# A graph network's two attention layers: one chain per chunk shared anew between ScalarE and VectorE, and the order of single steps moved

## The reference, cut to what matters

```python
h = jnp.maximum(_layernorm(x), 0.0)
x = x + _L0_gnn_ref(h, adj, embed, layer, embed_bias, layer_bias)
h = jnp.maximum(_layernorm(x), 0.0)
x = x + _L1_gnn_ref(h, adj, beta1, beta2)
# _L0_gnn_ref:
h = h_add(h_mul(x, embed), embed_bias)
neigh = exp_map_zero(adj @ log_map_zero(h))
out = h_add(h_mul(concatenate((x, neigh), 1), layer), layer_bias)
# _L1_gnn_ref, twice, _leaky after each:
x_norm = x / clip(norm(x), EPS)
attn = softmax(where(a > 0, beta[0] * (x_norm @ x_norm.T), NEG_INF))
h = attn @ x
```

## Time and profile before

| | us |
|---|---|
| runs shown | 993.46, 994.92, 997.03 |
| profiled execution | 993.61, its span 992.1 |
| TensorE busy | 935.3 (94%) |
| VectorE busy | 819.4 (83%) |
| ScalarE busy | 511.4 (52%) |
| fp32 products of the aggregation (L463) | 225.6 |

### The profile page before, as it was taken

How to read it: one execution, slowest core, us unless ns; L and a number is a source line. 1 busy time by engine, 2 the same in 40 slices (tenths; PEclk the granted TensorE clock), 3 DMA queues, 4 the chain that set the end, 5 groups by cost and what they waited for, 6 DMA issues and landing times.

```text
span 992.1 us, 22921 instructions
## 1 busy us (share of the span) xinstructions
PE 935.3 (94%) x9024; PEld 698.0 (70%) x9024; DVE 819.4 (83%) x2110; ACT 511.4 (52%) x708; POOL 8.0 (1%) x21
## 2 busy tenths in 40 slices
PE   2789999999997989999999999989999999999996
PEld 1754444444444878788888888768878888888885
DVE  7791888888888987788988898988768788888887
ACT  2720211211216575765656677777565565656564
POOL 0000000000000000000000000000000000000000
PEclk9879999999998999999999999999999999999999
DMA  8219888888881444555555655535655556555630
GB/s 343 94 62 312 278 284 277 278 286 298 275 275 43 168 174 177 207 210 219 211 200 195 244 206 192 183 145 187 238 183 212 211 193 245 213 204 205 252 139 36
DMA packets 29971, 207.26 MB, mean 209 GB/s; under 512 B 3632, under 2 KB 4272, under 8 KB 5296
## 3 DMA queue, kind: packets, MB, share of 16 engines
q1 hardware_dynamic: 28224, 203.44, 56.6%
q0 software_dynamic: 640, 2.10, 0.5%
q10 hardware_dynamic: 1008, 0.33, 0.1%
HBM read 203.75 MB, written 2.10 MB: 207 GB/s over the span
## 4 chain that ended last, share of the span: by engine, by line
PE 84%; DVE 8%; ACT 4%; issue 2%; DMA 1%; DVEq 0%; POOL 0%; SPq 0%; POOLq 0%; ACTq 0%
PE acc_ps L463 20%; PE s_ps L614 17%; PE s_ps L600 10%; PE acc_ps L667 6%; PE acc_ps L663 6%; PE acc_ps L665 6%; PE acc_ps L644 5%; PE acc_ps L640 5%; PE acc_ps L642 5%; PE acc_ps L427 1%; DVE work L1604 1%; ACT work L971 1%; DMA x_sb<-in_x 1%; ACT set L764 1%; PE s_ps L441 1%
## 5 line engine op out<-in xcount | busy, mean ns | idle before, releaser
L971 ACT ACTIVATE work<-s_ps,beta_bias,beta_scale 128x1024 f32<-128x1024 f32 x144 | 173.5, 1205 | 223.2 <-PE s_ps L614 223.2
L463 PE MATMUL acc_ps<-ring,set 128*128 128x512 f32 x512 | 225.6, 600 | 3.1 <-DVE set L1230 3.1
L1622 DVE SCALAR_TENSOR_TENSOR h_all<-ring,s_ps 128x1024 f32<-128x1024 f32 x112 | 136.6, 1220 | 69.9 <-PE s_ps L600 69.1
L463 PEld LDWEIGHTS acc_ps<-ring,set 128*128 128x128 f32 x512 | 97.3, 192 | 120.8 <-issue 117.8
L1604 DVE TENSOR_TENSOR work<-work 128x1024 f16<-128x1024 f32 x96 | 132.5, 1380 | 5.4 <-ACT work L981 5.4
L981 ACT ACTIVATE work<-work 128x1024 f16<-128x1024 f32 x96 | 131.5, 1369 | 3.1
L1612 DVE SCALAR_TENSOR_TENSOR work<-ring,work 128x1024 f32<-128x1024 f32 x96 | 116.7, 1215 | 0.0
L614 PE MATMUL s_ps<-xt 128*128 128x512 f16 x432 | 107.6, 385 | 6.3 <-ACT work L971 5.5
L614 PE MATMUL s_ps<-set 128*128 128x512 f16 x432 | 105.3, 379 | 2.6 <-ACT t L1029 2.1
L663 PE MATMUL acc_ps<-set,work 128*128 128x129 f16 x576 | 103.5, 220 | 4.6 <-DVE accs L1639 2.7
L663 PE MATMUL acc_ps<-src,work 128*128 128x129 f16 x576 | 102.9, 219 | 1.9 <-ACT accs L995 1.9
(11 more groups left out here) (254 smaller groups left out, 1726.1 us busy)
## 6 DMA issues: line engine op xcount, KB each, us to landing
ring<-in_adj_t SPq DMA_DIRECT2D x192, 1024.0 KB, 5.0
x_sb<-in_x SPq DMA_DIRECT2D x4, 512.0 KB, 7.3
out<-x_sb POOLq DMA_DIRECT2D x8, 256.0 KB, 2.5
w<-in_layer ACTq DMA_DIRECT2D x2, 64.0 KB, 8.7
w<-in_embed ACTq DMA_DIRECT2D x1, 64.0 KB, 4.2
eb<-in_embed_bias ACTq DMA_DIRECT2D x1, 64.0 KB, 7.0
lb<-in_layer_bias ACTq DMA_DIRECT2D x1, 64.0 KB, 11.3
beta<-in_beta ACTq DMA_DIRECT2D x2, 0.5 KB, 14.6
```

The costliest lines, as they stand in the source:

```text
L463: last = nc.tensor.matmul(agg, v_sb[:, jb, :], ring[:, k, b, :], start=jb == 0, stop=jb == NB - 1)
L971: nc.scalar.activation(values[x.n % VR], score_ps, ACT.Exp, bias=beta_bias[:, x.la:x.la + 1], scale=beta_scale[:, x.la:x.la + 1]).then_inc ...
L1622: V.scalar_tensor_tensor(turned[x.off % MR].rearrange("p (b j) -> p b j", b=CB), ring[:, x.mir_tile % AR, :, ds(x.h * HB * P, HB * P)], 0. ...
```

## The change

- **Row 0's total.** On ScalarE `first_total` moves ahead of the slot's exponential, and the `first_flush` of the same slot behind it.
- **Row 5** of the first attention layer is turned 11 slots after its last half, not 10.
- **Last chunk.** Its chain is cut for 12 pauses, its slots 0 and 1 stand ahead of its first Tanh on ScalarE, `chunk_scales` has a part of its own, the scaled rows come two slots later, and its columns are turned in slot 12, not 11.
- **Every chunk.** `gnn_chunk` uses the same functions as the last chunk: ScalarE does the squares of t1, relu and its squares, both scaled rows and the high halves, at the end of its part of the chunk; VectorE keeps the small steps and the low halves. VectorE's steps on its own semaphore go from 82 to 77 for each chunk, the asks from 5 to 7.
- **First stage.** The relu pass is gone; the transposes read scr_b, and the copy out of PSUM applies relu. The `gb` products come chunk by chunk behind `g`; `web` is made before the layer norm's scalars. SyncE waits for x before it loads the ring.

```diff
-        LAST_CHUNK_AT = 11
-        turned_at = {LAST_CHUNK_AT: (0, NC - 1), **{rows_of[a].last + 10: (1, a) for a in range(NC)}}
+        LAST_CHUNK_AT = 12
+        turned_at = {LAST_CHUNK_AT: (0, NC - 1), **{rows_of[a].last + (11 if a == 5 else 10): (1, a) for a in range(NC)}}
...
-        PAUSES = 11
-        ASKS_CHUNK = 5
+        PAUSES = 12
+        ASKS_CHUNK = 7
...
+            sp.wait_ge(x_in[XP - 1], 16)
...
             def h_transposes(r):
-                pe.wait_ge(h_ready, r + 1)
+                pe.wait_ge(xs_ready, r + 1)
                 wait(pe, ht_copied, r - 1)
                 for b in range(CB):
-                    last = nc.tensor.transpose(ht_ps[r % 2][:, ts(b, P)], h_sb[:, r * CB + b, :], ident[:, :])
+                    last = nc.tensor.transpose(ht_ps[r % 2][:, ts(b, P)], scr_b[:, r * CB + b, :], ident[:, :])
                 last.then_inc(ht_done, 1)
...
                     last = nc.tensor.matmul(g_ps[r % 2][:, b, :], ht_sb[:, ts(r * CB + b, P)], w1[:, 0:F],
                                             start=True, stop=True)
                 last.then_inc(g_done, 1)
-            pe.wait_ge(web_made, 1)
-            for b in range(NB):
-                last = nc.tensor.matmul(gb_ps[:, b:b + 1], ht_sb[:, ts(b, P)], web[:, :], start=True, stop=True)
-            last.then_inc(gb_done, 1)
+                if r == 0:
+                    pe.wait_ge(web_made, 1)
+                for b in blocks(r):
+                    last = nc.tensor.matmul(gb_ps[:, b:b + 1], ht_sb[:, ts(b, P)], web[:, :], start=True, stop=True)
+                last.then_inc(gb_done, 1)
...
-            relu(0)
             for r in range(NC):
-                if r + 1 < NC:
-                    relu(r + 1)
                 act.wait_ge(ht_done, r + 1)
-                nc.scalar.activation(ht_sb[:, ds(r * CH, CH)], ht_ps[r % 2], ACT.Copy).then_inc(ht_copied, 1)
+                nc.scalar.activation(ht_sb[:, ds(r * CH, CH)], ht_ps[r % 2], ACT.Relu).then_inc(ht_copied, 1)
                 if r:
                     g_out(r - 1)
...
                 on(ACT.Tanh, sm(5, CB), sm(4, CB))
                 if c_last(c):
                     split_columns(0, c - 1, xt_before_ps)
+                chunk_squares(dump)
                 log_terms(sm(4, CB), sm(5, CB), sm(6, CB))
                 if not first and not c_last(c):
                     split_columns(0, c - 1, xt_ps)
                 on(ACT.Tanh, sm(5, CB), sm(4, CB))
-                on(ACT.Copy, x_sb[:, ds(c * CB, CB), :], t1[:, :, :])
+                chunk_relu(c, dump)
+                chunk_rows(c)
+            def asked_for():
+                asks[1] += 1
+                act.wait_ge(asked, asks[0] + asks[1])
+            def chunk_squares(unused):
+                asked_for()
+                for b in range(CB):
+                    last = nc.scalar.activation(unused[:, b, :], t1[:, b, :], ACT.Square,
+                                                accum_out=small[:, 2, CB + b:CB + b + 1])
+                last.then_inc(told, 1)
+            def chunk_relu(c, unused):
+                asked_for()
+                for b in range(CB):
+                    last = nc.scalar.activation(t2[:, b, :], t1[:, b, :], ACT.Relu, bias=small[:, 3, b:b + 1])
+                last.then_inc(chunk_made, 1)
+                act.wait_ge(chunk_made, c * 2 + 1)
+                for b in range(CB):
+                    last = nc.scalar.activation(unused[:, b, :], t2[:, b, :], ACT.Square,
+                                                accum_out=small[:, 2, CB + b:CB + b + 1])
+                last.then_inc(told, 1)
+                nc.scalar.activation(x_sb[:, ds(c * CB, CB), :], t1[:, :, :], ACT.Copy)
+            def chunk_rows(c):
+                asked_for()
+                for b in range(CB):
+                    last = nc.scalar.activation(t2[:, b, :], t2[:, b, :], ACT.Copy, scale=small[:, 1, b:b + 1])
+                last.then_inc(chunk_made, 1)
+                act.wait_ge(chunk_made, c * 2 + 2)
+                for b in range(CB):
+                    last = nc.scalar.activation(t3[:, b, :], t2[:, b, :], ACT.Copy, scale=small[:, 9, b:b + 1])
+                last.then_inc(xn_ready[0], 1)
+                nc.scalar.activation(src[0][:, ds(c * CB, CB), F:2 * F], t2[:, :, :], ACT.Copy, scale=FS)\
+                    .then_inc(told, 1)
...
                 pause(-1)
+                pause(0)
                 on(ACT.Tanh, sm(5, CB), sm(4, CB))
                 split_columns(0, c - 1, xt_before_ps)
-                pause(0)
                 pause(1)
-                asked_for()
-                for b in range(CB):
-                    last = nc.scalar.activation(t3[:, b, :], t1[:, b, :], ACT.Square,
-                                                accum_out=small[:, 2, CB + b:CB + b + 1])
-                last.then_inc(told, 1)
+                chunk_squares(t3)
                 for i in (2, 3, 4):
                     pause(i)
                 log_terms(sm(4, CB), sm(5, CB), sm(6, CB))
...
+                chunk_relu(c, t3)
...
                 pause(10)
+                chunk_rows(c)
+                pause(11)
...
-                x = at(n - 4)
-                if x and x.off is not None and x.h == 1 and x.a == 0:
+                i, x = row_ending.get(n - 4), at(n - 4)
+                first = x and x.off is not None and x.h == 1 and x.a == 0
+                if i is not None and rows_of[i].a == 0:
+                    first_total(i)
+                elif first:
                     first_flush(x)
                 if at(n):
                     raise_scores(at(n))
-                i = row_ending.get(n - 4)
-                if i is not None and rows_of[i].a == 0:
-                    first_total(i)
+                if i is not None and first:
+                    first_flush(x)
                 if at(n):
                     high_halves(at(n))
                 if i is not None:
...
+            dve.wait_ge(embed_in, 16 * 2)
+            V.scalar_tensor_tensor(bsq[:, :], w1[:, 0:F], 1.0, eb[:, :], ALU.mult, ALU.mult,
+                                   accum_out=web[:, :]).then_inc(web_made, 1)
             step(ins)
...
-            dve.wait_ge(gb_done, 1)
+            dve.wait_ge(gb_done, NC)
...
                 product_scalars(small[:, 0, both], sm(2, CB), sm(9, CB), sm(10, CB), y2[:, 1:2], CB)
+                chunk_sum()
+                chunk_stats(c)
+                chunk_deviations()
+                chunk_scales()
+                chunk_low(c)
...
+            def chunk_product(w_in, c):
+                answered()
+                step(V.tensor_tensor(sm(3, CB), sm(5, CB), sm(1, CB), ALU.mult))
+                for b in range(CB):
+                    ins = V.scalar_tensor_tensor(t1[:, b, :], w_in[:, b, :], small[:, 3, b:b + 1],
+                                                 h1_sb[:, c * CB + b, :], ALU.mult, ALU.add)
+                ask(ins)
+                V.tensor_tensor(sm(7, CB), sm(3, CB), sm(3, CB), ALU.mult)
+            def chunk_bias(c):
+                for b in range(CB):
+                    ins = V.scalar_tensor_tensor(t2[:, b, :], t1[:, b, :], 1.0, lb[:, :], ALU.mult, ALU.mult,
+                                                 accum_out=small[:, 9, b:b + 1])
+                step(ins)
+                V.tensor_tensor(sm(7, CB), sm(7, CB), n_ps, ALU.mult).then_inc(w_read, 1)
+                dve.wait_ge(w_read, c + 1)
+                V.tensor_tensor(small[:, 2, 0:CB], sm(7, CB), hh[:, ds(c * CB, CB)], ALU.add)
+            def chunk_norms(c):
+                answered()
+                step(V.tensor_copy(sm(10, CB), small[:, 2, both]))
+                norm(sm(0, 2 * CB), sm(1, 2 * CB), squares, EPS, 2 * CB)
...
-                ask(V.tensor_tensor(t1[:, :, :], x_sb[:, rows, :], t1[:, :, :], ALU.add))
+            def chunk_stats(c):
+                step(V.tensor_tensor(t1[:, :, :], x_sb[:, ds(c * CB, CB), :], t1[:, :, :], ALU.add))
...
-                for b in range(CB):
-                    ins = V.tensor_scalar(t2[:, b, :], t1[:, b, :], mean_var[:, b, 0:1], None, ALU.subtract)
-                step(ins)
-                for b in range(CB):
-                    ins = V.scalar_tensor_tensor(t3[:, b, :], t2[:, b, :], 0.0, t2[:, b, :], ALU.max, ALU.mult,
-                                                 accum_out=small[:, 2, CB + b:CB + b + 1])
-                step(ins)
+                ask(V.tensor_scalar(sm(3, CB), mean_var[:, 0:CB, 0], -1.0, None, ALU.mult))
+            def chunk_deviations():
+                answered()
                 step(V.tensor_scalar(squares, squares, TINY, None, ALU.max))
                 inv_sqrt(sm(1, 2 * CB), squares, sm(3, 2 * CB))
-                for b in range(CB):
-                    ins = V.tensor_scalar(t2[:, b, :], t2[:, b, :], 0.0, small[:, 1, b:b + 1], ALU.max, ALU.mult)
-                step(ins)
-                V.tensor_tensor(sm(0, CB), small[:, 1, both], small[:, 2, both], ALU.mult)
```

(83 more changed lines are left out.)

78 lines of the change are left out of this document (13 added, 65 removed).

## The result

The changed kernel took 1014.12 us (median of four, 1012.48 to 1015.3) against 994.19 for the kernel before on the same chip: ratio 1.0194, interval 1.0167 to 1.0221. The forecast was 1011, with a range of 1002 to 1020. The profiled execution of after took 1013.28 us, 19.7 more than that of before; its span is 1011.7.

The account below looks back on a forecast made before the run. TensorE was taken to bound the aggregation, ScalarE and VectorE the stage before 61 us. Terms -1.9 + 18.2 + 3.6 + 5.1 - 8.8 = +16.2 us on 993.6 gave 1009.8, as median 1011; range 1002 to 1020.

Parts of the forecast that it names:

- first stage: Before the aggregation: shorter ScalarE loop without the relu pass and no wait for gb, -1.9 us.
- ring: Aggregation turns: copies, layer product, VectorE, ScalarE in a circle, 32.8 us from VectorE's start D against 29.7; +18.2 us.
- clock in the stalls: Aggregation: TensorE's clock falls in two of six stalls, slowing the layer product; +3.6 us, bounds 0 and 11.
- into the last chunk: Start of chunk 7's chain: D+34.6 instead of D+29.5, after a pause of about 5 us; +5.1 us.
- attention: Attention: total's waits -3.8, row 5's columns -3.5, last chunk's recut -1.5; -8.8 us in all.
- Rival 2: Aggregation: ring costs more, +7 us for the clock and 1 to 3 for loop jumps; 1020 us, chance 0.14.
- Rival 3: Aggregation: ScalarE's copies ready by D+27.7, turns stay 29.7 us, only gains remain; about 981 us, chance 0.11.
- Rival 4: Ring stands but the attention's gains fail because another wait ends as late; 1016 us, chance 0.12.
- rival 1: Aggregation: ring closes as said, but the clock stays up in all stalls; 1006 us, chance 0.18.

Follow-up runs that it names:

- e4: Changed kernel with ScalarE's two copies for the next chunk ahead of this chunk's scaled rows, and high halves ahead of the second scaled rows: 983.01 us, ratio 0.9885.
- e5: Changed kernel with two extra float32 products on TensorE filling most of each stall ahead of the wait for ScalarE's copies: 1010.25 us, ratio 1.0156.
- e1: Changed kernel with the chain of chunks 0 to 6 put back as in the kernel before: 983.63 us, ratio 0.989.
- e3: Changed kernel with only ScalarE's two copies for the next chunk moved ahead of this chunk's scaled rows: 990.31 us, ratio 0.996.
- e6: Changed kernel with the columns turned ahead of the second tile of the next aggregation instead of the fourth: 1008.99 us, ratio 1.0152.
- e8: Kernel before with only the first row's total copied ahead of the exponential and the flush behind it: 990.73 us, ratio 0.9954.
- e9: Kernel before with only row 5's columns turned eleven slots after the row's last half instead of ten: 992.08 us, ratio 0.9974.
- e7: Kernel before with the first stage's part of the change alone: 991.28 us, ratio 0.9976.
- e10: Kernel of e4 with 32 transposes of the identity on TensorE ahead of its first work: 983.36 us, ratio 0.9885.
- e2: Kernel before with only the changed chain of chunks 0 to 6: 1024.85 us, ratio 1.0311.

## Why the prediction was right, step by step

| step | worked out | in the profiled executions | in runs of the part alone |
|---|---|---|---|
| first stage | -1.9 | -2.2 | -3.4 (0.9 to 4.0 less) |
| ring | +18.2 | +18.1 | |
| clock in the stalls | +3.6 | +7.6 | |
| into the last chunk | +5.1 | +5.0 | |
| the three together | +26.9 | +30.7 | +30.0 |
| attention | -8.8 | -8.9 | total -3.8, row 5 -2.5 |
| sum | +16.2 | +19.6 | |

The third column is read at VectorE's first step of each chunk. The first of the eight was at 97.20 before and is at 95.02 now; the last came 207.2 us behind it before and comes 237.9 behind it now. From there to the end it is 687.7 and 678.8 us.

**First stage.** The size came out in the two profiled executions, by another route and partly by luck: the first aggregation product came at 60.12 in after, but at 58.03 in e4 and at 63.20 in e5, whose first stage is the same, against 61.43 before. The loop is not bound by ScalarE any more, as the prediction said, and steps at 2.18 us rather than 2.35. But the first two steps run at the lower clock and give much of it back: ScalarE's logarithm is ready at 42.87, no sooner than the 42.79 of the earlier trace rows, where 0.4 us sooner had been worked out. What is gained is the wait for `gb` (1.48 us, gone) and the start of the first aggregation, which begins at 60.12 rather than 61.43 and reaches full clock sooner.

**Ring.** Every piece is where it was worked out: the norms at D+6.5 (168.47), the squares answered at D+23.29 against 23.3, rows asked at D+26.5 against 26.7, layer product at D+30.84 against 30.85, and the turn at full clock 32.83 against 32.8. The experiments bear out the reason too: e1 takes the chain back and the 30 us go; e3 leaves all the work and moves only the copies, and 24 go; with e4's order 31 go (some 2 of them perhaps the first stage's clock).

**Clock, the term that was mis-sized.** It was put at two stalls of six, 1.8 us each. Three fell, at 2.46, 2.56 and 2.57 us: 7.6, which is above the 3.6 taken and below the bound of 11. The step that failed is the sentence "the slower tiles behind it eat only the pause". The slower tiles also bring the transposes of the columns 3.4 us later after the layer product, and ScalarE's copy of those columns stands in the middle of the chain, ahead of the second Tanh. So the lower clock entered the ring a second time. The 1.8 us a stall had been put at the layer product itself, and there it costs less: with its norms it lasts 0.74, 0.62 and 0.57 us longer in the three turns, since the clock fell in its middle; the other 1.7 to 2.0 of each are the late columns. e6 shows it: with the columns in time the same number of falls costs 1.2 us together, 1.0 of it by the one that took in the layer product; and e5: without the fall, no turn is long. These 4 us are the 3 by which 1011 fell short of 1014, less what the first stage gave beyond its term. What is left for the bare ring is 25.7 - 7.6 = 18.1.

**Into the last chunk.** 34.47 us from the start of chunk 6's chain to that of chunk 7's, where 34.6 had been worked out, with the stall of 5.02 us and the layer product at the lower clock, as expected.

**Attention.** The two waits on the first row's total went for 3.8 us, as worked out (2.8 to 6.3 by the interval). Row 5 gave 2.5 alone, with -3.5 taken: the wait of 2.12 shrank to 0.8, so the whole of it was not to be had. The last chunk's part has no run of its own, and its term stays open. The wait for low halves (L1604, L1579 in after) shrank by 1.1 at its longest, 3.0 to 1.9, where 1.5 had been taken. Those for the exponential, for which nothing was counted, fell by 3.7 in total, and a new one of 1.4 us for the masks (L1587) came. From the start of the last chunk's chain to the first row's averages it is 99.3 us in before and in e8, 97.9 in after and 98.6 in e1, but 101.0 in e9 and 99.6 in e5, which do not differ from before and from after in that stretch. A gain of 1.5 can't be told from such a scatter, and that the sum of -8.8 came out as -8.9 is in part luck.

**The rivals.** Rival 2, the ring with a dearer clock at 1020, was nearer to the truth in the clock (7 us) than the forecast, and wrong in the jumps: the loops add nothing that shows. Rival 3, ScalarE through before D+27.7, fell with the second copy at D+30.2. Rival 4 fell with e8 and e9, and rival 1 is what e5's turns look like.

## What to carry to other kernels

When work is handed from one engine to another, look at what the receiving engine does for a third one and whether the new work will stand ahead of it; the sum of busy time says nothing on that (ScalarE was 55% busy). Move the small step that another engine waits for ahead of the large one that waits itself: two copies moved were worth 24 us, and one fp16 pass moved some 5 to 7 more. A stall that brings the clock down is to be costed at every product that lies on the ring, including those that an engine in the chain waits for indirectly; turning the columns two tiles sooner (e6) took 6.3 us off six turns.

## What was not expected of the hardware

**The clock of TensorE's first steps decides how long the first stage is.** In the changed first stage, where TensorE is the bound of the loop, the transposes (L414) of the third and fourth chunk took 1.09 or 0.63 us, by the clock, other in each execution. In after:

```profile
23.93 1.09 PE L414 MATMUL acc_ps<-ident,xt 128*128 128x128 f32 x4
...
27.43 0.63 PE L414 MATMUL acc_ps<-ident,xt 128*128 128x128 f32 x4
```

In e4's profiled execution those of the third chunk already took 0.63, at 23.15; in e5's those of the fourth, at 28.91, still took 1.09, and the first v was ready at 63.20 rather than 60.12 (about 0.8 of it because x came later). A part of the spread between executions of one kernel may come from here: e7, which has this stage, gave eight times 989.8 to 992.1 and four times 994.9 to 995.3. That is argued and not shown, since one execution of each kernel has a trace, and e4 with the same stage spread by 0.9 us only.

**Transposes alone bring the upper clock.** The Trainium skill (TensorE: Matmul & The Clock Gate, "Part 4: PE-mode transpose") says that the full rate "doesn't engage" for transposes, since they don't count as busy in the same way. In e10 nothing but 32 fp32 transposes ran on TensorE ahead of 14.2 us. Those that ran between 10 and 12 us, and those between 13 and 14 (shortest, median and longest in ns, first and last start in us):

```profile
L418 PE MATMUL acc_ps<-ident x11: 421/421/421, 9.8 to 11.9; 128*128 128x128 f32 x11
L418 PE MATMUL acc_ps<-ident x11: 272/272/273, 12.8 to 13.9; 128*128 128x128 f32 x11
```

The starts are 0.21 us apart up to 12.55 and 0.11 from 12.84 on, half of it. That is the pace of the upper level: in after one group of four starts at 27.43 and the product behind it at 27.90, 0.118 each, where at the lower level it is 23.93 to 24.81, 0.22 each. So the trace doesn't agree with the page. (The column with the granted clock says 1.00 for all of that time, though in after the products between 20.57 and 22.36 ran at half pace, 2.00 us for eight where 1.06 is had; ahead of its first change the column is no guide, and the durations are.)

**The length of a stall doesn't tell whether the clock falls.** In after the stalls of 2.13, 2.87 and 2.88 us ahead of the layer product brought it down, and those of 1.97, 2.06 and 2.07 did not. That looks like a limit at 2.1 us, but other runs don't keep to it: in e2 a stall of 2.24 us at 159.54 left the clock up (the 24 products behind it took the 10.55 us of the upper level), and in e5 one of 1.16 us at 293.45 brought it down (12.19 us for the same 24), where three as long did not. The tiles behind the one in e2, and the layer product and the tiles in e5:

```profile
161.35 10.55 PE L465 MATMUL acc_ps<-ring,set 128*128 128x512 f32 x24
```

```profile
293.45 1.16 PE L445 MATMUL s_ps<-w,accs 128*128 128x128 f32 x8 [1.16 <-ACT accs L805]
...
295.31 12.19 PE L467 MATMUL acc_ps<-ring,set 128*128 128x512 f32 x24
```

Nor does the layer product alone tell: in e6 two of the three falls came behind it and show only in the tiles that follow. The falls had to be counted in the traces, and in advance they could only be bounded.
